# GpSimd makes a weight chunk's low parts in eight pieces of 128 columns instead of two of 512

## The reference

```python
xn = layernorm(x)
x  = x + attention(xn, Wq, Wk, Wv, Wo, We) + moe(xn, gate_w, w1, b1, w2, b2)
```

## Time and profile before

| | us |
|---|---|
| median of 3 runs | 715.39 |
| lowest and highest of them | 712.84, 716.93 |
| span of the profiled execution | 791.5 |
| stage 1, steps 0 to 15, in the profile | 82 to 337 |
| experts in the profile | 337 to 537 |
| stage 3 in the profile | 565 to 773 |

### The profile page before, as it was taken

How to read it: one execution, slowest core, us unless ns; L and a number is a source line. 1 busy time by engine, 2 the same in 40 slices (tenths; PEclk the granted TensorE clock), 3 DMA queues, 4 the chain that set the end, 5 groups by cost and what they waited for, 6 DMA issues and landing times.

```text
span 791.5 us, 24553 instructions
## 1 busy us (share of the span) xinstructions
PE 671.2 (85%) x7800; PEld 433.1 (55%) x7800; DVE 619.4 (78%) x1106; ACT 538.9 (68%) x1123; POOL 467.2 (59%) x542
## 2 busy tenths in 40 slices
PE   0477888989889896969999999996689989988886
PEld 0463344444444443559999999993244444444444
DVE  8989878878778785948888888885587888887871
ACT  2581566776667685858888888884466766766765
POOL 8650656666566555306555565656676676676671
PEclk9997899999999998999999999999699999999998
DMA  9779545665455653664555454443376666566632
GB/s 262 253 212 299 138 125 146 154 175 158 117 159 148 176 155 100 174 111 90 101 105 102 96 109 102 103 89 100 77 153 161 159 165 166 152 161 161 159 92 61
DMA packets 162947, 113.32 MB, mean 143 GB/s; under 512 B 72624, under 2 KB 150448, under 8 KB 162864
## 3 DMA queue, kind: packets, MB, share of 16 engines
q1 hardware_dynamic: 153632, 90.63, 46.2%
q0 software_dynamic: 8192, 16.86, 8.6%
q10 hardware_dynamic: 1040, 4.76, 1.6%
HBM read 55.42 MB, written 47.19 MB: 130 GB/s over the span
## 4 chain that ended last, share of the span: by engine, by line
PE 71%; DVE 7%; issue 7%; SPq 5%; ACT 4%; another core or an unknown queue 3%; DMA 1%; ACTq 0%; DVEq 0%
PE bank L1133 20%; PE bank L1111 13%; PE bank L1251 12%; PE mx L1240 12%; PE mx L1145 7%; ACT A L708 4%; DVE mx L956 2%; PE bank L1193 2%; PE bank L1031 2%; PE bank L1162 2%; DVE A L791 2%; PE bank L1155 1%; SPq L319 1%; SPq L318 1%
## 5 line engine op out<-in xcount | busy, mean ns | idle before, releaser
L708 ACT ACTIVATE A<-bank 128x512 f32<-128x512 f32 x502 | 279.1, 602 | 109.9 <-PE bank L1133 94.1
L956 DVE TENSOR_REDUCE mx<-mx 128x4 f16<-128x1024 f32 x256 | 303.7, 1208 | 56.3 <-PE mx L1145 26.8
L1133 PE MATMUL bank<-stack 113*128 113x256 f16 x1004 | 185.2, 283 | 51.2 <-issue 24.9
L565 POOL DMA_INDIRECT slots_x<-rows,pos x128 | 123.5, 965 | 91.3 <-PE bank L1133 68.0
L579 POOL TENSOR_SCALAR rows<-rows,slot_p 128x128 f32<-128x128 f32 x142 | 112.1, 798 | 103.4 <-DVE rows L1007 103.4
L609 POOL DMA_INDIRECT rows<-slots_y,pos x128 | 121.5, 950 | 73.4 <-PE bank L1133 54.6
L1133 PEld LDWEIGHTS bank<-stack 113*128 113x128 f16 x1004 | 66.9, 99 | 164.9 <-issue 85.7
L1111 PE MATMUL bank<-A,V 128*32 128x256 f32 x2048 | 142.2, 397 | 1.7 <-ACT A L708 1.6
L752 ACT ACTIVATE rows<-mx,b 128x256 f32<-128x256 f32 x284 | 111.8, 474 | 30.0 <-PE mx L1240 30.0
L1001 DVE TENSOR_TENSOR rows<-rows 128x512 f16<-128x512 f32 x142 | 101.2, 714 | 25.2 <-ACT rows L756 22.8
L1251 PE MATMUL bank<-w,rows 128*128 x1704 | 108.2, 220 | 4.4 <-DVE rows L1001 4.4
(11 more groups left out here) (142 smaller groups left out, 616.8 us busy)
## 6 DMA issues: line engine op xcount, KB each, us to landing
stack<-ctx_rest SPq DMA_DIRECT2D x64, 256.0 KB
stack<-qk_dram SPq DMA_DIRECT2D x128, 96.0 KB
slots_y<-rows SPq DMA_DIRECT2D x71, 128.0 KB, 2.0
qk_dram<-hi_qk SPq DMA_DIRECT2D x64, 128.0 KB
stack<-ctx_high SPq DMA_DIRECT2D x128, 64.0 KB
slots_x<-A ACTq DMA_DIRECT2D x1, 4644.0 KB, 20.2
w_stage<-in_w SPq DMA_DIRECT2D x8, 512.0 KB
qk_dram<-lo_qk SPq DMA_DIRECT2D x64, 64.0 KB
```

The lines of the kernel that those rows point to most:

```text
L565: pool.indirect_dma_start(slots_x, bass.IndirectOffsetOnAxis(pos[j][:, t:t + 1], 0), rows[:, t, :].bitcast(F32), None).then_inc(s_scat, 16)
L708: act.activation(A[:, n % NA, :, :].rearrange("p h s -> p (h s)"), scores(k, n)[:, :], ACT.Exp, scale=SCALE).then_inc(s_xp, 1)
L956: dve.tensor_reduce(mx[:, a, 8 * qt:8 * qt + 8].rearrange("q (i e w) -> q i e w", i=2, e=2)[:, :, g % 2], MX[u % 2][:, :].rearrange("q (i ...
L1133: mm = pe.matmul(scores(k, n)[:, i * S:(i + 1) * S], stack[0:SHIFT + 1, par, h, 1, c * P:(c + 1) * P], stack[0:SHIFT + 1, par, h, 0, :], s ...
```

## The change

A constant `LP = 8` takes the place of 2 for the number of pieces. GpSimd subtracts 128 columns at a time. The first piece of chunk c may stand behind a scatter that waits for at least 16 (2c+2) + 9 scores, and each of the next seven behind the next scatter; pieces that find no scatter follow the last one. The counts that SyncE and TensorE wait for, and the last chunk's increments on VectorE, follow.

```diff
+LP = 8
...
-                    sp.wait_ge(s_wlo, 2 * c + 2)
+                    sp.wait_ge(s_wlo, LP * (c + 1))
...
-            def low_half(c, h):
-
-                cols = slice((2 * c + h) * WCH // 2, (2 * c + h + 1) * WCH // 2)
+            def low_piece(c, h):
+
+                cols = slice((LP * c + h) * WCH // LP, (LP * c + h + 1) * WCH // LP)
                 pool.wait_ge(s_wsc, c + 1)
-                pool.tensor_tensor(w12[:, 1, cols], w_stage[:, h * WCH // 2:(h + 1) * WCH // 2], w12[:, 0, cols], ALU.subtract).then_inc(s_wlo, 1)
+                pool.tensor_tensor(w12[:, 1, cols], w_stage[:, h * WCH // LP:(h + 1) * WCH // LP], w12[:, 0, cols], ALU.subtract).then_inc(s_wlo, 1)
...
-                    c_lo, h_lo = n_low // 2, n_low % 2
-                    if c_lo < NCH - 1 and n_ex >= 16 * (2 * c_lo + 2) + 8 + 3 * h_lo:
-                        low_half(c_lo, h_lo)
+                    c_lo, h_lo = n_low // LP, n_low % LP
+                    if c_lo < NCH - 1 and n_ex >= 16 * (2 * c_lo + 2) + 9:
+                        low_piece(c_lo, h_lo)
                         n_low += 1
-            assert n_low == 2 * (NCH - 1)
+            for n in range(n_low, LP * (NCH - 1)):
+                low_piece(n // LP, n % LP)
...
-                            dve.scalar_tensor_tensor(out=w12[:, 1, cols], in0=w_stage[:, h * WCH // 2:(h + 1) * WCH // 2], scalar=FS, in1=w12[:, 0, cols], op0=ALU.mult, op1=ALU.subtract).then_inc(s_wlo, 1)
+                            dve.scalar_tensor_tensor(out=w12[:, 1, cols], in0=w_stage[:, h * WCH // 2:(h + 1) * WCH // 2], scalar=FS, in1=w12[:, 0, cols], op0=ALU.mult, op1=ALU.subtract).then_inc(s_wlo, LP // 2)
...
-                        for sm, n in ((s_red, 8 * (HALF + 1)), (s_wlo, 2 * NCH)):
+                        for sm, n in ((s_red, 8 * (HALF + 1)), (s_wlo, LP * NCH)):
```

## The result

The changed kernel takes **741.6 us** (median of 4 runs, 739.03 to 743.85), the kernel before 714.12 us (4 runs, 712.81 to 716.93). The ratio is 1.038, with a 95% interval of 1.0351 to 1.0409: slower by 27.5 us, where the forecast was 3.0 and its range ended at 725.

What follows compares the result with a forecast made beforehand. TensorE was taken as the bound, GpSimd following it. Late `load` plus transfer, less slack, gave TensorE waits of 1 to 4 us, taken as 3; other terms zero: 715.4 + 3.0 = 718.4 us, range 713 to 725.

Steps and rivals of the forecast that it cites:

- price of a piece: GpSimd, stage 1: one subtraction of 128 columns takes 0.40 us, bounds 0.29 and 0.58.
- slot: GpSimd, stage 1: a scatter, its piece and the gaps take 1.58 us together.
- slack: Start of even steps: a `load` can land 1.4 us later before TensorE waits, bounds 0.6 to 2.3.
- GpSimd keeps up, with 0.2 us to spare: Stage 1: scatters are released every 1.77 us, a scatter with its piece takes 1.58, so pieces do not pile up.
- 5 us of nothing to do: SyncE in step 3: idle gap between the load of `w_stage` at 133.01 and the next `load` at 138.17.
- counted like the others: Chunk 5 (step 13): taken to cost the same as the other chunks, with no special stop.
- The late `load`: SyncE, mid odd step: the `load` behind `w_stage` goes out 0.1 to 0.2 us late, 1.0 in chunk 1, 0 in chunk 2.
- The transfer in front: DMA engines: the moved 512 KB of `w_stage` make the `load` behind it end 1.2 us later, between 0.9 and 1.4.
- B: ScalarE at the high part: waits for a late `w_stage` and becomes the bound, +9 us, 724; chance 0.19.
- A: Start of even steps: all lateness is hidden by a slack of 2 us or more, 715.4; chance 0.18.
- C: Start of odd steps: moving the `w_stage` transfer away removes stops there, up to 6 us faster, 709; chance 0.08.
- D: VectorE, stage 1: halves keep it from running, so splitting frees up to 10.8 us, some 4 of them; chance 0.05.

Runs made afterwards that it cites:

- e1: The kernel before with nothing edited, run again for a second profile: 712.63 us (one run), profiled span 710.9 us.
- e2: Against the kernel before: eight pieces of 128 columns per chunk, four behind each of the two scatters where the halves stood; 714.04 us, ratio 0.9999.
- e6: Against the changed kernel: four pieces of 256 columns behind four scatters instead of eight of 128; 714.49 us, ratio 0.9995.
- e7: Against the changed kernel: the eight pieces of a chunk begin at 6 scores instead of 9; 719.49 us, ratio 1.0073.
- e9: Against the kernel before: SyncE's first `load` of each of 14 steps of stage 1 waits for two scores more; 721.17 us, ratio 1.0086.
- e10: Against the changed kernel: the eight pieces of a chunk begin at 4 scores instead of 9; 715.25 us, ratio 1.0003.
- e4: Against the changed kernel: SyncE's load of `w_stage` moves 128 columns instead of 1024, its wait kept; 724.3 us, ratio 1.014.
- e8: Against the changed kernel: the eight pieces of a chunk begin at 12 scores instead of 9; 758.76 us, ratio 1.0605.
- e5: Against the changed kernel: GpSimd sends the load of `w_stage` on its own queue behind the eighth piece, instead of SyncE; 735.19 us, ratio 1.0296.

## Why the prediction was wrong, point by point

**The place was right.** What counts is SyncE's load of `w_stage`, which waits for the last piece and has the `load` of the next step behind it; TensorE then waits ahead of the first plain product of the even steps. The price of a piece (0.40 forecast, 0.436 measured) and of a slot (1.58, 1.62), the zero for GpSimd's extra work, the zero for VectorE, and the unchanged stage 3 and experts stand. The slack (1.4, measured 1.0 to 1.2) was good.

**The step that failed is "GpSimd keeps up, with 0.2 us to spare".** Its 1.77 us between releases came from a score of 0.99 us, read from one step of the first profile. Scaled by the ratio of whole spans, 0.90, it gave 1.6, "still just keeps up". But that profile's extra time lay unevenly: the undisturbed score is 0.82 us, and a release comes every 1.8 x 0.82 = 1.47 us, against a slot of 1.62. GpSimd loses 0.15 us in each slot, over seven slots some 1.1 us, and the two scores of head start that most chunks have are worth 1.6 us instead of 2.0. So the buffer, forecast free some 0.5 us before the middle of the step (in chunk 1 as much after it), came free 0.64 to 1.50 us past it in five chunks and 3.85 in chunk 5. The same pace left SyncE's gap of "5 us of nothing to do" at 128.68 - 126.36 - 0.36 = 2.0 us in e1.

**Chunk 5 was not like the others.** In the changed kernel GpSimd stood for 2.76 us ahead of the scatter that carries its seventh piece, and without that its last piece would have come some 1.3 us past the middle, much as in the other chunks. The trace names a score product, but no late score explains it. The same scatter, which waits for score 212, stands in e1 too, and starts there 3 us after SyncE has sent the `load` that waits for score 216 (GpSimd's row, then SyncE's):

```profile
265.43 0.96 POOL L565 DMA_INDIRECT slots_x<-rows,pos  x1 [5.39 <-PE bank L1133]
```

```profile
262.21 0.33 SPq L326 DMA_DIRECT2D stack<-ctx_rest  x1
```

It stands in the profile that the prediction was read from as well (5.15 us, start at 297.28), so "counted like the others" could have been seen to fail. In the kernel before, in e2, e6, e7, e9 and e10 the last piece of chunk 5 is done ahead of it; in the changed kernel, e4 and e8 it is not. e5 alone has no such stop (0.16 us). What the scatter waits for stays open.

**The late `load`.** Forecast 0.1 to 0.2 us in four chunks, 1.0 in chunk 1, none in chunk 2: 1.6 us in all. Measured from the eighth exponential: 2.3, 2.3, 1.5, 1.6, 1.5 and 4.3, less the 0.14 that e1 has too, 12.6 us in all. This is the largest error.

**The transfer in front** was forecast at 1.2 us. e4 shows 1.7 for seven eighths of it, so some 2 us for the whole. The full 1.4 that 512 KB take at 377 GB/s would have been short too. e5 has TensorE wait 4.9 us for `stack` behind the transfers although they are no longer in SyncE's queue and the `load` goes out on time, so not all of it is the place in one queue. How much comes from that place and how much from transfers that run at the same time, no run here tells apart.

**A term that was missing: the clock.** The prediction charged a late load once, by the microsecond. Each of TensorE's six stops behind a late `load` in the changed kernel (2.33 to 4.71 us) was followed by a stretch at a granted clock of 0.50, together worth 8.8 us net in the busy time of stage 1.

With the measured terms the prediction's sum gives 12.6 + 6 x 2.0 - 6 x 1.2 = 17.4 us of stops, where 19.2 were counted, and with 8.8 for the clock 26 to 28; measured 27.5, and 28.9 between the two profiles. The split is good to some 3 us, since the busy time of matmuls in a profile is modelled (e9's, at a whole clock, is 2.4 us below e1's for the same products).

**The rivals.** *B* named a mechanism that is there: ScalarE waited 5.4 us for `w_stage`. But in chunks 0 and 3, where it waited for nothing, TensorE stopped for 2 us and more all the same, so it is not what bounds the changed kernel; with the `load` out of its way, in e5, it is the larger of TensorE's waits (7.5 us against 6.4). Its 724 was too low for the same lateness that sank the forecast. *A* (hidden) needed a slack of 2 us, and e9 shows 1.0 to 1.2; e10 hides all of it for another reason, a buffer that is free before the middle. *C* fell: the stops at the start of odd steps belong to the first profile; e1 has none. *D*, in which a half keeps VectorE from running, fell with e2: shorter instructions win nothing (ratio 0.9999). Slower had 0.35, and its highest bound was some 10 us, because no case took the buffer to come free well after the middle.

## What to carry to other kernels

A buffer that is freed in small steps, each hung on some other work, is freed at the pace of that work: before hanging them up, compare the slot with the releases at the pace of an undisturbed profile, look for places where that work stands still, and look at who is queued behind the one that waits for the last step. A pace read from a profile whose span is 10% above the timed median can't be scaled by that ratio, since the extra time may lie in a few places. And a stop of TensorE is charged twice where the granted clock falls behind it, as here (19.2 us of stops, and 8.8 us of busy time behind them): read the clock in the microseconds after it.

## What was not expected of the hardware

Four subtractions of 128 columns in a row take 1.58 us on GpSimd in e2, 0.40 each, while one alone behind a scatter takes 0.44 and the scatter behind it follows after 0.17 us, where a scatter behind a scatter follows after 0.30. So a piece of 0.44 us costs GpSimd only 1.62 - 1.27 = 0.35 us of its pace (scatters alone come every 1.27 us when they lag, as at 124.24, 125.52 and 126.79 in e1's timeline). What a piece costs the kernel lies in its moment alone. And stops of TensorE of up to 1.0 us left the clock at 1.00 fourteen times in e9, while behind one of 1.36 and 0.31 us in e4 it fell to 0.50, and behind one of 1.86 us it did not.
